# Fewer row gathers underway for tiles 16 to 38, and two GpSimd score blocks placed later in the gather loop

## The reference, cut to what matters

```python
h = (x @ W.T).reshape(n, h_, d_)              # 384 nodes, 8 heads of 64
h_src = h[src]                                # one row of h for each edge
e = jax.nn.leaky_relu(e_src + e_dst, 0.2)
e = e * (1.0 + et_emb[edge_type])
e = e * edge_weight[:, None]
e_max = jnp.zeros((n, h_), x.dtype).at[dst].max(e)
e = jnp.exp(e - e_max[dst])
...
msg = h_src * alpha[:, :, None]
out = jnp.zeros((n, h_, d_), x.dtype).at[dst].add(msg).reshape(n, h_ * d_)
```

## Time and profile before

| | |
|---|---|
| median of 3 runs | 1761.28 us (1760.88 to 1765.62) |
| the profiled execution, its own time | 1765.62 us |
| its span | 1763.8 us |
| busy in the span: PE, DVE | 1650.7, 884.7 us |
| busy in the span: POOL, ACT | 647.2, 501.0 us |
| software DMA queue (q0) | 18592 packets, 29.91 MB |
| the L2 layer's GpSimd loop, first to last gather | 1081.20 to 1244.49 us |

### The profile page before, as it was taken

One profiled execution on the slowest core, in us unless ns is written; L12 is line 12 of the kernel. 1 busy time (PEld: TensorE's weight loads), 2 busy tenths in 40 slices (PEclk: granted clock), 3 DMA queues, 4 the chain that ended last, 5 costly groups with the idle time before them and its releaser, 6 DMA issues.

```text
span 1763.8 us, 23533 instructions
## 1 busy us (share of the span) xinstructions
PE 1650.7 (94%) x7303; PEld 934.1 (53%) x7304; DVE 884.7 (50%) x2161; ACT 501.0 (28%) x1586; POOL 647.2 (37%) x756
## 2 busy tenths in 40 slices
PE   6989999999899999999999898797899999999898
PEld 4534444445655645555555766542444555555555
DVE  8878888878834443244254147885622101101322
ACT  1134444447431413223231125210200121111234
POOL 5867788773232323333341812677200000000000
PEclk9999999999999999999998998899999999999899
DMA  8030101105414223232216653556335221220020
GB/s 318 1 105 25 61 25 36 44 14 133 129 49 129 78 81 93 58 82 64 77 45 131 232 181 120 157 166 170 99 114 178 72 77 57 92 77 6 19 54 18
DMA packets 119614, 161.76 MB, mean 92 GB/s; under 512 B 49497, under 2 KB 61721, under 8 KB 119154
## 3 DMA queue, kind: packets, MB, share of 16 engines
q1 hardware_dynamic: 93056, 115.43, 20.9%
q0 software_dynamic: 18592, 29.91, 6.3%
q10 hardware_dynamic: 7890, 15.44, 2.6%
HBM read 145.26 MB, written 15.47 MB: 91 GB/s over the span
## 4 chain that ended last, share of the span: by engine, by line
PE 83%; DVE 10%; DMA 3%; issue 2%; ACT 2%; POOL 0%; ACTq 0%; DVEq 0%; POOLq 0%
PE psum L373 81%; DVE stats L470 1%; DVE arena L2688 1%; DMA ring<-tab_h,sd_t 1%; DVE ring L1299 1%; DMA arena<-tab_h,sd_t 0%; DVE xn L2067 0%; PE psum L1028 0%; DVE xn L2073 0%; DMA arena<-tab_x 0%; ACT xT L414 0%; DMA x<-in_x 0%; DVE xn L2086 0%; ACT arena L2954 0%; PE psum L2302 0%
## 5 line engine op out<-in xcount | busy, mean ns | idle before, releaser
L373 PE MATMUL psum<-arena,ring 128*128 (+1 forms) x1504 | 325.8, 363 | 9.7 <-issue 6.2
L373 PE MATMUL psum<-arena 128*128 128x384 f32 (+9 forms) x1804 | 313.0, 328 | 18.8 <-DVE arena L2688 5.7
L373 PE MATMUL psum<-xT,ring 128*128 128x384 f32 x928 | 310.9, 495 | 7.2 <-ACT xT L414 4.2
L373 PE MATMUL psum<-ring,arena 128*128 128x512 f32 (+1 forms) x570 | 261.5, 604 | 11.8 <-DVE ring L666 6.9
L373 PEld LDWEIGHTS psum<-arena 128*128 128x128 f32 (+5 forms) x1804 | 192.7, 152 | 146.0 <-issue 71.2
L373 PEld LDWEIGHTS psum<-xT,ring 128*128 128x128 f32 x928 | 178.3, 194 | 133.7 <-issue 17.9
L373 PE MATMUL psum<-ring,xT 128*128 128x512 f32 x552 | 247.0, 599 | 1.7 <-issue 0.7
L373 PEld LDWEIGHTS psum<-arena,ring 128*128 128x128 bf16 (+1 forms) x1504 | 139.1, 115 | 131.4 <-issue 30.0
L1079 ACT ACTIVATE ring<-ring 128x128 f32<-128x128 f32 x416 | 123.3, 297 | 173.5 <-DVE ring L1365 173.5
L373 PEld LDWEIGHTS psum<-ring,arena 128*128 128x128 f32 (+1 forms) x570 | 99.2, 187 | 135.7 <-issue 134.7
L373 PEld LDWEIGHTS psum<-ring,xT 128*128 128x128 f32 x552 | 103.4, 192 | 121.8 <-issue 118.6
(11 more groups left out here) (478 smaller groups left out, 1731.4 us busy)
## 6 DMA issues: line engine op xcount, KB each, us to landing
ring<-in_L_ffn_w SPq DMA_DIRECT2D x22, 1024.0 KB, 8.0
ring<-in_L_gnn_m_w SPq DMA_DIRECT2D x8, 1024.0 KB, 5.8
ring<-in_L_ffn_expert_weights SPq DMA_DIRECT2D x8, 1024.0 KB, 5.5
ring<-tab_key ACTq DMA_DIRECT2D x24, 256.0 KB, 3.2
ring<-in_L_gnn_Wv SPq DMA_DIRECT2D x5, 1024.0 KB, 5.2
tab_w<-xn SPq DMA_DIRECT2D x6, 768.0 KB, 14.7
ring<-in_L_gnn_Ww SPq DMA_DIRECT2D x4, 1024.0 KB, 17.4
ring<-in_L_gnn_wq SPq DMA_DIRECT2D x4, 1024.0 KB, 5.3
```

The costliest lines, as they stand in the source:

```text
L373: return nc.tensor.matmul(o, a, b, start=start, stop=stop)
```

## The change

Two things change, both in what GpSimd does and when. The gathers 16 to 38 wait for tile T - 2 instead of tile T - 3; from T = 39 (`GR`) on the rule is as before. The first score block is called ahead of gather 12 instead of gather 7, and the second ahead of gather 19 instead of gather 12. The groups in each block, the instructions and the waits of the other engines stay.

```diff
-        WIDER, UNDERWAY = 16, (2, 3)
+        UNDERWAY = (2, 3)
...
-                most = UNDERWAY[T >= WIDER]
+                most = UNDERWAY[T >= GR]
                 if T >= most:
                     row_landed(pool, T - most)
...
-        POOLED_SCORES = {7: (0, 9), 12: (9, 16)}
+        POOLED_SCORES = {12: (0, 9), 19: (9, 16)}
```

## The result

The changed kernel takes 1778.52 us in the median of five runs (1775.53 to 1782.0). The ratio to the kernel before is 1.0083, 95% interval 1.0065 to 1.0101, so it is 0.83% slower, 14.6 us on the median of before. The two medians themselves lie 17.2 us apart. The forecast was 9.7 us, or 0.55%. The profiled execution has a span of 1783.1 us and was the slowest execution of this kernel. It is 19.3 us longer than the profiled one of before, and over half of that did not come back when the change was run again.

What follows compares the result with a forecast made beforehand. GpSimd's gather loop was taken as the bound, with about 19 us slack on DVE and PE. Moved blocks cost nothing and the narrower queue 9.7 us, put on the median: 1771.0 us, 0.55% slower, range 1764.5 to 1777.

Steps and rivals of the forecast that it cites:

- The bound: At the end of the L2 layer, GpSimd's gather loop sets the end; its last gather decides when layer norm may start.
- The slack of about 19 us: DVE and PE in the gather stage: with all rows there, PE would finish near 1231 instead of 1250.
- the 9.9 us that were laid on it: Delay of DVE's L2701 waiting for moved block 2, putting the first multiply near 1145; costed at nothing.
- The buffers are no limit: Gather loop: gather 97 needs only tile 58 finished, and PE has done 64 tiles long before it goes out.
- Part 1: Score blocks moved in GpSimd's order: block 2 ends at 1126.0, GpSimd some 2 us late at tile 19, DVE's delay free.
- Part 2: Two underway up to tile 38: gathers 19 to 37 at 1.90 us each, tile 39 at 1163.0, 9.7 us late.
- that of the tiles behind 39: Gathers from tile 39 on: pace of 1.57 us holds, so the last gather goes out at 1254.2.
- the sign of a wrong forecast: Gather loop: the forecast is wrong if the last gather is late by much less than tile 39 is.
- Rival 1: Gather loop: the narrower queue costs nothing, only moved blocks up to 2 us remain, 1761 to 1763; chance 0.13.
- Rival 2: DVE and PE become the bound, block 2's wait shows in full: 1771.2, or 1774 if both add; dearer form 0.05.
- Rival 3: Gathers of the second half: late DVE no longer holds them, saving 18.6 us, net -8.9, 1752; chance 0.06.

Runs made afterwards that it cites:

- e3_blocks_only_again: Second run of moving only the score blocks, to gathers 12 and 19, against the kernel before: 1764.94 us, ratio 0.9983.
- e1_control: Kernel before with only SyncE's two first-layer count waits rewritten to a bounds-checking load, far from the change: 1768.79 us, ratio 1.0004.
- e2_blocks_late: Only the score blocks moved, to gathers 12 and 32, three underway from tile 16, against the kernel before: 1774.84 us, ratio 1.0069.
- e3_four_from_7: Four gathers underway from tile 7 on, blocks at 7 and 12, against the kernel before: 1803.54 us, ratio 1.0216.
- e1_narrow_only: Only the rule of two underway extended to tile 38, blocks left at 7 and 12, against the kernel before: 1775.4 us, ratio 1.0039.
- e1_blocks_only: Only the score blocks moved, to gathers 12 and 19, three underway from tile 16, against the kernel before: 1766.84 us, ratio 0.9996.
- e2_narrow_all: Two gathers underway for all 98 tiles, blocks left at 7 and 12, against the kernel before: 1810.65 us, ratio 1.0261.

## Why the prediction was right, and where its sizes were off

**The bound.** GpSimd's loop sets the end, DVE and PE have slack: right, and shown by three kernels. Multiplies that start 7 to 18 us late are free (e3_blocks_only_again, e1_control), 24 us late cost 12 us (e2_blocks_late). The slack of about 19 us was near enough for the 9.9 us that were laid on it, but another limit comes first.

**"The buffers are no limit".** Right for the changed kernel, but the buffers are what ends the slack. Gather 39 waits for tile 0, and in e1_control, e2_blocks_late and e3_four_from_7 it starts 2.5 us after the first multiply. In the kernel before, it started 1153.26 - 1135.03 = 18.2 us after it. So a first multiply more than 18.2 - 2.5 = 15.7 us late puts gather 39 off. The measured delays of gather 39 fit: 17.6 - 15.7 = 1.9 us in e1_control and 24.2 - 15.7 = 8.5 us in e2_blocks_late. The 1.9 us were made good by the last multiply.

**Part 1.** Times of the blocks and of L2701 were right within 0.5 us, and so was the cost of nothing. The gathers ahead of block 1 were not as close: gather 7 went out at 1096.38, not 1098.3, since gather 5 had gone out earlier (1092.27 instead of 1094.49). One item was wrong: DVE did not reach L2698 1 us sooner but 4.3 us later (1120.07 instead of 1115.75), and waited that much less for block 2. The moved blocks need not be the cause: with the blocks where they were, L2698 started at 1120.96 in e1_control and at 1120.82 in e1_narrow_only. The end of stage 1 scatters by some 5 us between executions.

**Part 2.** The pace of 1.90 was 1.87 to 1.91 from gather 19 to 31 in the four profiles of the narrow rule up to tile 38 (1.89 to 1.96 from 19 to 37 in the three without the long hold), and tile 39 was 9.4 to 11.2 us late in three of four, against 9.7. The term that was off is that of the tiles behind 39. I held it at the 1.57 us of the one profiled execution; all but one of the later profiles with three underway there have 1.51 to 1.56, and that one (1.66) holds the gather of 7.84 us. The last multiply was thus 6.7 to 7.6 us late in these three, 2.7 to 4.0 us less than tile 39. That is partly the sign of a wrong forecast that I had named, a last gather that is late by less than tile 39 is. By the ratios of three measurements the change costs 0.37 to 0.83%, and the forecast of 0.55% lies among them. By the ratio the first measurement stands at 1775.9 us, inside the range of 1764.5 to 1777; its plain median of 1778.52 lies 1.5 us above the range. That the mean of the ratios (0.59%) falls so near the forecast is in part luck, since the stage accounts for only 7 to 8 us in the profiles.

**The first measurement's excess over the forecast.** In the profile it is two gathers, 5.7 us, and 5 us of F2 at a lower clock. Neither was there in the two further profiles of the change. Both turned up once elsewhere, a long hold in e1_blocks_only (7.84 us) and the longer F2 in e1_narrow_only. So they come and go with the execution; what sets them off is open. They are read from one profiled execution, and how much of the 14.6 us they make up in the other executions is not shown.

**Rival 1** (two underway cost nothing) is refuted by the dose: 0, 12 and 23 more gathers at the narrow pace put gather 39 off by 0, 4.9 and 9.4 us, and 82 of them cost 46 us. The rival needed landings of 2.7 us; the shortest in e2_narrow_all is 3.1 us.

**Rival 2** (DVE and PE become the bound) did not come in at the 9.5 us of the changed kernel. What it says of the buffers came true beyond 15.7 us.

**Rival 3** (faster) had its mechanism right and its trigger wrong. Gathers that share a landing with a multiply are held by it, as e2_narrow_all shows row by row. A late DVE does not part them; a fourth gather underway does, though the multiplies then stretch the issue itself (pace 1.40, not 1.25).

## What to carry to other kernels

When a chain of indirect gathers sets the end of a stage, its length is the count times the pace. With two underway the pace was (landing + restart) / 2, the restart being the time from a landing to the next issue: 1.82 us with a restart of 0.24, and about 2.0 of the measured 2.10 with one of 0.74. With more underway this is only a lower bound. For three it gives (3.7 + 0.24) / 3 = 1.31 us and the loop took 1.46 and 1.57, since VectorE's operations hold the issue too. The issuing engine's own floor was 1.25 us. Anything that delays the consumers is free up to their slack, and the slack can end at a buffer rather than at the consumers' own work, so weigh late work on the issuing engine by what it does to the chain, not by the wait it makes elsewhere. But more underway is not better without end: with one step more the other engines may stall, so change the number by one, and look at the idle times of engines that have nothing to do with the gathers.

## What the runs showed of the hardware

**A gather's issue is held by VectorE's two-input float32 operations, if these have begun first.** In the changed kernel DVE's L651 runs from 1230.92 for 1.08 us, and the gather issued beside it takes 1.80 us instead of 0.94:

```profile
1230.92 1.08 DVE L651 TENSOR_TENSOR arena<-iota,ranking 128x896 f32<-128x896 f32 x1
```

```profile
1229.58 0.94 POOL L630 DMA_INDIRECT arena<-tab_h,sd_t  x1 [0.50 <-PE psum L373]
1231.03 1.80 POOL L630 DMA_INDIRECT arena<-tab_h,sd_t  x1 [0.50 <-PE psum L373]
```

All eight gathers of e2_narrow_all that began 0.10 or 0.11 us into an L651 took 1.80 us. In the kernel before, a gather took 1.59 us when it began 0.31 us into an L651, 1.29 us when 0.62 us into it, and 0.95 us when it began 0.31 us ahead of it. DVE, then GpSimd:

```profile
1170.82 1.09 DVE L651 TENSOR_TENSOR arena<-iota,ranking 128x896 f32<-128x896 f32 x1 [1.39 <-PE psum L373]
1177.61 1.09 DVE L651 TENSOR_TENSOR arena<-iota,ranking 128x896 f32<-128x896 f32 x1 [0.24 <-PE psum L373]
1205.77 1.08 DVE L651 TENSOR_TENSOR arena<-iota,ranking 128x896 f32<-128x896 f32 x1
```

```profile
1171.44 1.29 POOL L630 DMA_INDIRECT ring<-tab_h,sd_t  x1 [0.53 <-issue]
1177.30 0.95 POOL L630 DMA_INDIRECT ring<-tab_h,sd_t  x1 [0.30 <-issue]
1206.08 1.59 POOL L630 DMA_INDIRECT xT<-tab_h,sd_t  x1 [0.30 <-issue]
```

The 0.71 us distance to the multiplies says the same. The Trainium skill (SBUF — State Buffer, the port rules for VectorE and GpSimd) has it that a `tensor_tensor` with both inputs in SBUF contends only with what GpSimd reads, and infers that descriptor generation is spared. The measurement decides here: with this indirect DMA, the issue is not spared. The gather reads its row numbers from `sd_t`, which lies in SBUF, so it may be this read that is held, as the page's rule on reads would have it. No run separates the two.

**Other engines stall when gathers flow without a pause.** Idle times of 5.6 to 24 us on PE, DVE and ACT, with no releaser, appeared in the control with three underway and grew with four from tile 7 and with five. With four from tile 16 no wait of PE, DVE or ACT without a named releaser is over 1.9 us in the stage. The cause is open. The Trainium skill (Runtime: NRT & Kernel Launch, "Instruction fetch mechanics") says that engines fetch their instructions by DMA in blocks of 16 KiB. A fetch underway through such a stall would look like this, but the traces speak against it. While ACT stood from 1128.08 to 1152.14 in e3_four_from_7, the gathers' queue was the only one with packets. The DMA queues in the window 1128 to 1152 (packets, MB, share):

```profile
q0 software_dynamic: 1538, 5.05, 74.0%
```

The last packet of an instruction queue ahead of it ended at 1115.93, the next began at 1156.03, when ACT was at work again. In e1_control there was none between 1126.42 and 1157.90, around all of its stalls.

**The same program scatters by 22 us** on one chip (1759.28 to 1781.81, 33 executions) and by 11 us over 16 on another. A change of half a per cent needs its reference on the same chip, and its stages compared in the profiles.
